# Two-layer GNN on one core: segment maxima subtracted by TensorE, scans in PSUM, and a regrouped division between the layers

## The chip, the cores and the metric

The kernel runs on one core of one Trainium2 chip. The metric is device time in microseconds (us). A core has TensorE (PE), VectorE (DVE), ScalarE (ACT), GpSimd (POOL) and SyncE (SP), each with its own instruction queue. They work on SBUF and PSUM and meet only through semaphores. Here SP issues the plain DMAs, and POOL issues the indirect ones (gathers of rows by an index list).

## The reference, cut to what matters

The graph has 6250 nodes with 128 numbers each and 106250 edges sorted by destination. Layer 0 is a softmax aggregation, separately for each of the 128 channels:

```python
h = maximum(layernorm(x), 0)
msg = h[src] + edge_attr                  # (106250, 128)
s = msg * beta
m = segment_max(s, dst)                   # (6250, 128)
e = exp(s - m[dst])
agg = segment_sum(msg * e, dst) / segment_sum(e, dst)
x = x + (agg @ H(phm_rule, W) + bias) + h
```

Layer 1 is a graph attention layer on `h = maximum(layernorm(x), 0)`: `Wx = h @ W.T` in 4 heads of 32, a logit for each edge and head, a softmax over each destination's edges, the weighted sum of `Wx[src]`, an elu, and a residual.

## The kernel before

Edges are taken in 208 groups of 512 (NG = 208, GE = 512, four blocks of 128). Each engine runs its own software pipeline over the groups (`sweep_edges`); a stage is listed with a lag, and the stages of one step stand on the engine's queue in the order of the list. An engine executes its queue strictly in order.

**Layer 0.** POOL issues four gathers a group (`gather0`, line 586) of `h` rows from DRAM into one of four ring buffers `ring_h`; it may run ahead until the ring is full (it waits for `lifted` of four groups back). ACT (merge0 lag 5, lift0 lag 0, weigh0 lag 3) copies the rows to PSUM (`lift0`, line 703), takes the exponentials of two groups of numbers from `bank[2]` (`weigh0`, lines 688 and 691), and merges finished sums into `acc` (`merge`, lines 666 to 674). DVE (add0 0, one_hot0 0, products0 3, maxima0 1) adds the rows to the edge attributes (line 950), builds a one-hot matrix (line 976), multiplies weights and messages (line 967), and finds segment maxima. For the maxima the messages stand transposed in PSUM (channels on partitions, edges along the row), and two scans run over them in `segment_max`: one forward (line 929) into `run_max`, one reversed (line 932) into `seg_max`, each with the flags of segment starts as its other tensor; line 939 takes the step between groups (`drop`), and line 960 subtracts the maxima from the messages into `diff`. PE (sums0 4, turn0 0, unturn0 2) transposes the messages by a product with `beta_ident` (`turn0`, line 1188), transposes `diff` back into `bank[2]` (`unturn0`, line 1197), and forms the segment sums by 16 multiplications with the one-hot matrices (`segment_sums`, line 1179). The merge of a group must end before the sums of the next may start.

An f32 multiplication of 128x128 by 128x128 appears in the records as two MATMULs. The lines of the trace speak of those halves, a row "x8" is four of them.

**Between the layers.** `acc` holds numerators and denominators for all nodes. In 13 batches of 512 nodes (the last has 106), ACT takes Ln of the denominator and twice Exp of the negative (`seed0`, lines 715 to 718), to PSUM and to SBUF; POOL multiplies that first guess of the reciprocal by the denominator (`polish0`, line 597); DVE makes the Newton step and multiplies by the numerator (`divide0`, lines 1008 and 1010); PE multiplies by the weight matrix on top of the bias (`layer_out`, lines 1219 and 1223; the bias is split in three bf16 parts by lines 991 to 999 on DVE); DVE adds to the nodes and takes statistics (`finish0`, lines 1019 and 800), two batches behind. `norm_all_nodes` then computes all reciprocal roots in Newton steps on DVE (lines 809 to 822), the same function as in the preamble. After it ACT normalizes, PE multiplies, and SP stores the table that layer 1 gathers from.

**Layer 1** has the same structure. `segment_max` is shared; there its data are 4 rows (heads) in PSUM and its forward scan writes to PSUM (`sums`).

Of the kernel before, what the change touches and what calls it, by code (L numbers as in the profile page):

```python
# [20 lines left out]
BF16 = mybir.dt.bfloat16  # L21
I32 = mybir.dt.int32
ALU = mybir.AluOpType
ACT = mybir.ActivationFunctionType

P = 128
# [44 lines left out]
def gnn_kernel(nc, x_in, src_in, dst_in, ea_in, rule_in, w0_in, bias_in, beta_in, w1_in, a_in, out):  # L71
# [31 lines left out]
    with ctx:  # L103
# [23 lines left out]
        head_pick = sb("head_pick", [P, H])  # L127
        junk = sb("junk", [1, 1])
# [3 lines left out]
        bias_parts = sb("bias_parts", [P, GB, D], BF16)  # L132
        ones_parts = sb("ones_parts", [P, P], BF16)
# [52 lines left out]
        run_max = sb("run_max", [P, 2, GE])  # L186
# [9 lines left out]
        bias_hi, bias_mid, bias_lo = (hn[:, 0, i, :].bitcast(BF16)[:, 0:D] for i in range(3))  # L196
        bias_rest = hn[:, 1, 0, :]
# [55 lines left out]
        bias_step = sem("bias_step")  # L253
        bias_made = sem("bias_made")
# [3 lines left out]
        mid_inv = sem("mid_inv")  # L258
# [77 lines left out]
        def _(sp):  # L336
# [122 lines left out]


# [11 lines left out]
            def load1(g, s, use):  # L472
                if s % HALF == 0:
                    load_lists(g, s, use, L1)
# [39 lines left out]
        def _(pool):  # L514
# [32 lines left out]
            pool.memset(ones_parts[:, :], 1.0).then_inc(self_pool, 1)  # L547
# [44 lines left out]
            def polish0(b):  # L592
                w = LAST if b == NBAT - 1 else GE
                pool.wait_ge(mid_seed, b + 1)
                if b >= 2:
                    pool.wait_ge(mid_inv, b - 1)
                pool.tensor_tensor(diff[:, b % 2, 0:w], acc[:, 1, b * GE:b * GE + w], ring_h[:, b % HRING, 0:w], ALU.mult  # L597
                                   ).then_inc(mid_near, 1)

            straight(NBAT, [(0, polish0)])  # L600
# [26 lines left out]
        def _(act):  # L627
# [25 lines left out]

            def merge(g, s, use, k, read_out, where=own_sums):
# [50 lines left out]
            sweep_edges(act, [(5, merge0), (0, lift0), (3, weigh0)])  # L705
# [3 lines left out]

            def seed0(b):  # L710
                w = LAST if b == NBAT - 1 else GE
                if b >= HRING:
                    act.wait_ge(mid_out, b - HRING + 1)
                near = ring_h[:, b % HRING, 0:w]
                act.activation(near, acc[:, 1, b * GE:b * GE + w], ACT.Ln).then_inc(mid_log, 1)
                act.wait_ge(mid_log, b + 1)
                act.activation(bank[b % HRING][:, 0:w], near, ACT.Exp, scale=-1.0)
                act.activation(near, near, ACT.Exp, scale=-1.0).then_inc(mid_seed, 1)

            straight(NBAT, [(0, seed0)])  # L720
# [63 lines left out]
        def _(dve):  # L784
# [21 lines left out]
            def norm_all_nodes():  # L806
# [52 lines left out]
            def h0(b, u, use):  # L859
                if u in DVE_SLOTS:  # L860
# [7 lines left out]
                    for t in range(GB):  # L868
                        ins = dve.tensor_scalar(run_max[:, 0, t * D:(t + 1) * D],
# [4 lines left out]
                    lnx = run_max[:, 0, :].rearrange("p (t d) -> p t d", d=D)  # L874
# [22 lines left out]

            dve.tensor_scalar(beta_ident[:, :], ident[:, :], beta[:, 0:1], None, ALU.mult).then_inc(beta_ready, 1)
# [18 lines left out]
            def segment_max(g, s, use, k, n, data):  # L917
                par = s % 2
                run = run_max[0:n, par, :] if k is L0 else head_run
                run_end = run_max[0:n, 1 - par, GE - 1:GE] if k is L0 else seg_max[0:n, 1 - par, GE - 1:GE]  # L920
# [10 lines left out]
                dve.wait_ge(k["scanned"], 2 * g + 1)  # L931
                dve.tensor_tensor_scan(seg_max[0:n, par, ::-1], flag[:, GE:0:-1], run[:, ::-1], -BIG,  # L932
# [21 lines left out]
            def maxima0(g, s, use):  # L954
                par = s % 2
                dve.wait_ge(L0["msgT"], g + 1)
                segment_max(g, s, use, L0, P, bank[par][:, :])
# [386 lines left out]
```

## Time and profile before

| | us |
|---|---|
| median of 3 runs | 2346.74 (2345.33 to 2385.2) |
| the profiled execution, its own time | 2345.14 |
| its span in the profile | 2343.4 |
| busy: PE / DVE / ACT / POOL | 1771.0 / 2109.2 / 1384.5 / 1644.0 |
| mean granted PE clock | 0.948 of full speed |

The profile is of one execution. Its times are us unless marked ns. PE is TensorE's multiplications and PEld its weight loads; SPq is a queue of SP. A line such as L586 is a line of the kernel before. In the lines of the trace, "busy" is the sum of a group, then comes the mean of one in ns, then the idle time of the engine just before them and what ended it; "issue" is idle time in which the engine waited for nothing that the profile shows. POOL's records of indirect DMAs are the time that it takes to issue them, not the transfer. Layer 0's gathers run from 67 to 1133 us, the piece between the last merge and the last statistics from 1155.3 to 1216.5, and layer 1's from 1251 us on.

### The profile page before, as it was taken

How to read it: one execution, taken by the hardware profiler on the slowest of the kernel's cores; microseconds unless marked ns; L12 is line 12 of the kernel's file. 1: busy time of each engine (PE TensorE's matmuls, PEld its weight loads, DVE VectorE, ACT ScalarE, POOL GpSimd, SP SyncE). 2: the span in 40 equal slices, each digit the busy share in tenths (PEclk: the TensorE clock that was granted, in tenths of full speed). 3: DMA queues.
4: the chain of work that ended last, by engine and by line, in shares of the span. 5: the costliest groups of instructions: out<-in, count | busy, mean ns of one | idle time of the engine just before them, and what ended most of it. 6: DMA issues, size and time to landing. Idle time of an engine off the chain costs nothing.

```text
span 2343.4 us, 60995 instructions
## 1 busy us (share of the span) xinstructions
PE 1771.0 (76%) x14105; PEld 1632.4 (70%) x14106; DVE 2109.2 (90%) x4081; ACT 1384.5 (59%) x3509; POOL 1644.0 (70%) x1728
## 2 busy tenths in 40 slices
PE   0466666666666666666557999999999999999996
PEld 0466666666666666666447888888888888888885
DVE  5799999999999999999666988889888888888887
ACT  2266666666666666666783555555555555555555
POOL 3677777777777777777314777777777777777772
PEclk9999999999999999999857999999999999999998
DMA  4544444444444444444003333333333333333332
GB/s 126 146 128 129 133 125 127 129 129 132 128 133 128 124 128 133 128 132 129 23 0 96 62 60 59 59 59 59 58 59 59 58 59 59 58 59 58 59 60 66
DMA packets 338882, 214.19 MB, mean 91 GB/s; under 512 B 170832, under 2 KB 305339, under 8 KB 338828
## 3 DMA queue, kind: packets, MB, share of 16 engines
q0 software_dynamic: 53248, 112.57, 20.8%
q1 hardware_dynamic: 285580, 101.01, 16.9%
q8 instruction: 22, 0.36, 0.1%
q14 instruction: 32, 0.26, 0.0%
HBM read 201.38 MB, written 10.30 MB: 90 GB/s over the span
## 4 chain that ended last, share of the span: by engine, by line
POOL 49%; issue 22%; DVE 14%; DMA 7%; PE 3%; ACT 2%; SPq 1%; POOLq 1%; DVEq 1%; ACTq 0%
POOL msg L608 26%; POOL ring_h L586 23%; DMA ring_h<-h_dram,meta_g 5%; DVE seg_max L932 3%; DMA msg<-wx_dram,meta_g 2%; DVE sums L929 2%; DVE run_max L929 2%; PE sums L1179 1%; DVE onehot L913 1%; DVE prod L967 1%; DVE msg L950 1%; DVE onehot L976 1%; DVE prod L1083 1%; ACT sums L703 1%; POOL diff L597 1%
## 5 line engine op out<-in xcount | busy, mean ns | idle before, releaser
L608 POOL DMA_INDIRECT msg<-wx_dram,meta_g x832 | 790.5, 950 | 292.6 <-issue 246.9
L586 POOL DMA_INDIRECT ring_h<-h_dram,meta_g x832 | 812.6, 977 | 259.5 <-issue 257.7
L1179 PE MATMUL sums<-onehot,prod 128*128 128x128 f32 x3312 | 690.3, 292 | 27.0 <-ACT acc L674 11.8
L1179 PE MATMUL sums<-onehot,wgt 128*128 128x128 f32 x3312 | 671.0, 286 | 0.0
L1179 PEld LDWEIGHTS sums<-onehot,prod 128*128 128x128 f32 x3312 | 531.9, 202 | 73.6 <-issue 71.3
L1179 PEld LDWEIGHTS sums<-onehot,wgt 128*128 128x128 f32 x3312 | 533.5, 203 | 0.0
L1188 PE MATMUL banks<-beta_ident,msg 128*128 128x128 f32 x1664 | 244.4, 291 | 342.8 <-DVE msg L950 342.8
L1188 PEld LDWEIGHTS banks<-beta_ident,msg 128*128 128x128 f32 x1664 | 204.6, 194 | 383.2 <-DVE msg L950 332.4
L674 ACT ACTIVATE acc<-sums 128x1022 f32 x412 | 421.6, 1023 | 0.1
L703 ACT ACTIVATE sums<-ring_h 128x512 f32<-128x512 f32 x208 | 125.2, 602 | 385.4 <-DMA ring_h<-h_dram,meta_g 385.3
L929 DVE TENSOR_TENSOR_SCAN sums<-flags,seg_max,banks 4x512 f32<-4x512 bf16 x207 | 264.0, 1276 | 5.2 <-PE banks L1277 3.7
L929 DVE TENSOR_TENSOR_SCAN run_max<-flags,run_max,banks 128x512 f32<-128x512 bf16 x207 | 263.4, 1272 | 0.0
L932 DVE TENSOR_TENSOR_SCAN seg_max<-flags,run_max 128x512 f32<-128x512 bf16 x208 | 254.7, 1224 | 7.1
L932 DVE TENSOR_TENSOR_SCAN seg_max<-flags,sums 4x512 f32<-4x512 bf16 x208 | 251.1, 1207 | 7.1
L666 ACT ACTIVATE carried<-acc,scale 128x2 f32 x414 | 120.9, 292 | 177.2 <-PE sums L1179 162.2
L1268 PEld LDWEIGHTS banks<-window,onehotT 128*128 128x128 f32 x1664 | 211.7, 199 | 3.4 <-ACT onehotT L751 2.8
L1268 PE MATMUL banks<-window,onehotT 128*128 128x4 f32 x1664 | 205.7, 247 | 2.2 <-DMA window<-wx_dram 2.2
L739 ACT ACTIVATE sums<-logit_d 128x16 f32<-128x16 f32 x208 | 39.0, 188 | 263.0 <-DVE logit_d L1075 262.0
L913 DVE TENSOR_SCALAR onehot<-iota_f,meta_g 128x128 f32<-128x128 f32 x832 | 182.7, 279 | 5.8 <-DMA meta_g<-meta 5.7
L950 DVE TENSOR_TENSOR msg<-msg,sums 128x512 f32<-128x512 f32 x208 | 141.1, 678 | 15.1 <-ACT sums L703 14.8
L967 DVE TENSOR_TENSOR prod<-sums,msg 128x512 f32<-128x512 f32 x208 | 141.9, 682 | 1.8 <-ACT sums L691 1.8
L976 DVE TENSOR_TENSOR onehot<-banks,meta_g 128x512 f32<-128x512 f32 x208 | 142.5, 685 | 0.0
(166 smaller groups left out, 2667.0 us busy)
## 6 DMA issues: line engine op xcount, KB each, us to landing
msg<-in_edge_attr SPq DMA_DIRECT2D x207, 256.0 KB, 2.9
flags<-flag_dram SPq DMA_DIRECT2D x52, 512.2 KB
ring_h<-h_dram,meta_g POOLq DMA_INDIRECT x832
msg<-wx_dram,meta_g POOLq DMA_INDIRECT x832
window<-wx_dram SPq DMA_DIRECT2D x832, 2.0 KB
wx_dram<-msg SPq DMA_DIRECT2D x13, 272.0 KB, 2.4
nodes<-in_x SPq DMA_DIRECT2D x4, 768.0 KB, 8.2
h_dram<-wgt SPq DMA_DIRECT2D x12, 256.0 KB, 2.2
```

The source lines that it names most:

```text
L586: pool.indirect_dma_start(hg[:, s % HRING, b, :], None, h_dram, bass.IndirectOffsetOnAxis(ap=meta_g[:, s, b:b + 1], axis=0)).then_inc(L0[" ...
L608: pool.indirect_dma_start(msg[:, s, b, :], None, wx_dram, bass.IndirectOffsetOnAxis(ap=meta_g[:, s, b:b + 1], axis=0)).then_inc(L1["gather ...
L674: act.activation(acc[:, :, bass.ds(node + 1, WIN - 1)], where[:, :, 1:WIN], ACT.Copy).then_inc(k["merged"], 1)
L913: ins = dve.tensor_scalar(onehot[:, s, b, :], iota_f[:, :], key[:, b:b + 1], None, ALU.is_equal)
L929: dve.tensor_tensor_scan(run, flag[:, 0:GE], data, before, ALU.add, ALU.max).then_inc(k["scanned"], 1)
L932: dve.tensor_tensor_scan(seg_max[0:n, par, ::-1], flag[:, GE:0:-1], run[:, ::-1], -BIG, ALU.add, ALU.max).then_inc(k["scanned"], 1)
L950: dve.tensor_tensor(msg[:, s, :, 0:D], msg[:, s, :, 0:D], row_psum.rearrange("p (b d) -> p b d", b=GB), ALU.add).then_inc(L0["added"], 1)
L967: dve.tensor_tensor(prod[:, s % 2, :, :], wgt_psum.rearrange("p (b d) -> p b d", b=GB), msg[:, s, :, 0:D], ALU.mult).then_inc(L0["multipli ...
L976: dve.tensor_tensor(onehot[:, s, :, :], steps, key, ALU.is_equal).then_inc(L0["onehots"], 1)
L1179: ins = pe.matmul(where[:, j, bass.ds(off, P)], what[:, slot, b, :], onehot[:, s, b, :], start=(b == 0), stop=(b == GB - 1), skip_group_ch ...
L1188: ins = pe.matmul(bank[s % 2][:, b * P:(b + 1) * P], msg[:, s, b, 0:D], beta_ident[:, :], start=True, stop=True)
L1268: ins = pe.matmul(bank[1][:, b * H:(b + 1) * H], onehotT[:, s % 2, b * P:(b + 1) * P], window[:, s, b, :], start=True, stop=True)
```

## The change

In layer 0 the forward scan writes in place over the transposed messages in PSUM, the reversed scan reads them there, and `diff` on DVE is gone. PE forms `beta * msg - maxima` itself in `bank[2]`: one multiplication of `beta_ident` with all 512 columns of messages, and four of the maxima with a negated identity added to it. Between the layers ACT takes the logarithms of batches 0 to 3 in one go, then their exponentials, then the logarithms of the other nine, then theirs, and copies POOL's product to PSUM; POOL multiplies twice a batch (denominator and numerator by the guess), DVE makes one instruction a batch, and the weight matrix is negated. The bias is added to the nodes by POOL, in 13 instructions after its last gather. One Ln on one number is issued ahead of the last merge. The Newton steps have three instructions in place of four. SP's first list for layer 1 is loaded at the end of layer 0.

```diff
@@ segment_max (DVE, both layers)
-                run = run_max[0:n, par, :] if k is L0 else head_run
-                run_end = run_max[0:n, 1 - par, GE - 1:GE] if k is L0 else seg_max[0:n, 1 - par, GE - 1:GE]
+                run = data if k is L0 else head_run
+                run_end = seg_max[0:n, 1 - par, GE - 1:GE]
...
                 dve.wait_ge(k["scanned"], 2 * g + 1)
+                if k is L0 and later(g, 2):
+                    dve.wait_ge(L0["unturned"], g - 1)
                 dve.tensor_tensor_scan(seg_max[0:n, par, ::-1], flag[:, GE:0:-1], run[:, ::-1], -BIG,
@@ maxima0 (DVE)
-                segment_max(g, s, use, L0, P, bank[par][:, :])
-                if later(g, 2):
-                    dve.wait_ge(L0["unturned"], g - 1)
-                dve.tensor_tensor(diff[:, par, :], bank[par][:, :], seg_max[:, par, :], ALU.subtract
-                                  ).then_inc(L0["shifted"], 1)
+                segment_max(g, s, use, L0, P, bank[s % 2][:, :])
@@ turn0, unturn0 (PE)
-                    pe.wait_ge(L0["shifted"], g - 1)
+                    pe.wait_ge(L0["scanned"], 2 * g - 2)
...
-                pe.wait_ge(L0["shifted"], g + 1)
                 if later(g, 1):
                     pe.wait_ge(L0["weighed"], g)
+                pe.matmul(bank[2][:, :].rearrange("p (b d) -> p b d", b=GB), beta_ident[:, :], msg[:, s, :, 0:D],
+                          start=True, stop=False, skip_group_check=True)
+                pe.wait_ge(L0["scanned"], 2 * g + 2)
                 for b in range(GB):
-                    ins = pe.transpose(bank[2][:, b * P:(b + 1) * P], diff[:, s % 2, b * P:(b + 1) * P], ident[:, :])
+                    ins = pe.matmul(bank[2][:, b * P:(b + 1) * P], seg_max[:, s % 2, b * P:(b + 1) * P], neg_ident[:, :],
+                                    start=False, stop=(b == GB - 1), skip_group_check=True)
@@ layer_out (PE)
-                pe.matmul(sums[0:rows, b % 2, 0, 0:t * D], ones_parts[:, 0:rows],
-                          bias_parts[:, 0:t, :].rearrange("p t d -> p (t d)"), start=True, stop=False, skip_group_check=True)
...
-                                    ring_h[:, b % HRING, i * P:i * P + rows], phm[:, :, :].rearrange("p j b -> p (j b)"),
-                                    start=False, stop=(i == t - 1), skip_group_check=True)
+                                    ring_h[:, b % HRING, i * P:i * P + rows], phm_neg[:, :], start=True, stop=True)
@@ POOL, after its last gather0 (waits for the nodes of the first residual), in place of polish0
+            def add_bias(b):
...
+                pool.tensor_tensor(tiles, tiles, bias_all[:, :].rearrange("p (a d) -> p a d", a=1).to_broadcast([P, t, D]),
+                                   ALU.add).then_inc(bias_added, 1)
+            straight(NBAT, [(0, add_bias)])
+            def near0(b):
...
+                pool.wait_ge(mid_seed, b + 1)
+                if b >= 2:
+                    pool.wait_ge(mid_lifted, b - 1)
+                pool.tensor_tensor(diff[:, b % 2, 0:w], acc[:, 1, b * GE:b * GE + w], seed, ALU.mult).then_inc(mid_near, 1)
+                pool.wait_ge(mid_near, b + 1)
+                pool.tensor_tensor(seed, acc[:, 0, b * GE:b * GE + w], seed, ALU.mult).then_inc(mid_quot, 1)
@@ ACT, end of layer 0 and between the layers, in place of seed0
-            sweep_edges(act, [(5, merge0), (0, lift0), (3, weigh0)])
+            sweep_edges(act, [(5, merge0), (0, lift0), (3, weigh0)], until=NG + 4)
+            act.activation(spare[:, :], spare[:, :], ACT.Ln)
+            last(merge0, 0)
...
+            def log0(b):            # Ln of acc[:, 1] into free buffers
+            def seed0(b):           # waits mid_log, and mid_out of batch b - 4; Exp(-log) into ring_h
+            def lift_near0(b):      # waits mid_near, and mid_agg of batch b - 4
+                act.activation(bank[b % HRING][:, 0:w], diff[:, b % 2, 0:w], ACT.Copy).then_inc(mid_lifted, 1)
+            for b in range(HRING):
+                log0(b)
+            for b in range(HRING):
+                seed0(b)
+            for b in range(HRING - 1):
+                lift_near0(b)
+            for b in range(HRING, NBAT):
+                log0(b)
+            lift_near0(HRING - 1)
+            for b in range(HRING, NBAT):
+                seed0(b)
+                if b > HRING:
+                    lift_near0(b - 1)
+            lift_near0(NBAT - 1)
@@ DVE, between the layers, in place of divide0
+            def quotient0(b):
...
+                dve.scalar_tensor_tensor(rows, bank[b % HRING][:, 0:w], 2.0, rows, ALU.subtract, ALU.mult).then_inc(mid_agg, 1)
@@ norm_all_nodes (DVE), three times
-                    link(dve.tensor_tensor(t, y, y, ALU.mult))
+                    link(dve.scalar_tensor_tensor(t, y, -0.5, y, ALU.mult, ALU.mult))
                     link(dve.tensor_tensor(t, t, v, ALU.mult))
-                    link(dve.tensor_scalar(t, t, -0.5, 1.5, ALU.mult, ALU.add))
-                    link(dve.tensor_tensor(y, y, t, ALU.mult))
+                    link(dve.scalar_tensor_tensor(y, t, 1.5, y, ALU.add, ALU.mult))
@@ SP, after layer 0's loads
+            sp.wait_ge(L0["onehots"], NG)
+            for q in range(HRING):
+                sp.wait_ge(L0["gathered"][q], 64 * (NG // HRING))
+            load_lists(0, 0, 0, L1)
```

## Rows read from the trace of the kernel before

**Rows 1.** The page: busy time, share of the span, and instructions.

```profile
PE 1771.0 (76%) x14105; PEld 1632.4 (70%) x14106; DVE 2109.2 (90%) x4081; ACT 1384.5 (59%) x3509; POOL 1644.0 (70%) x1728
```

**Rows 2.** Windows: stretch, length, engines' busy time, granted clock, DMA share, GB/s.

```profile
67.00:1133.00 1066.00, 714.49 (x5722) 660.91 (x5723) 1033.77 (x1444) 661.96 (x1628) 812.64 (x832) 1.00 0.46 128
1155.30:1216.50 61.20, 28.72 (x111) 23.59 (x111) 35.17 (x88) 55.45 (x65) 13.46 (x13) 0.53 0.00 0
1251.00:2343.00 1092.00, 987.53 (x8002) 913.92 (x8002) 959.30 (x2332) 619.97 (x1693) 798.16 (x838) 0.92 0.32 59
```

**Rows 3.** Lines of layer 0, 67 to 1133 us: busy, mean ns, idle before.

```profile
L586 POOL DMA_INDIRECT ring_h<-h_dram,meta_g x832 | 812.6, 977 | 259.5 <-issue 257.7 <-ACT sums L703 1.8
L929 DVE TENSOR_TENSOR_SCAN run_max<-flags,run_max,banks 128x512 f32<-128x512 bf16 x204 | 259.6, 1272 | 0.0
L932 DVE TENSOR_TENSOR_SCAN seg_max<-flags,run_max 128x512 f32<-128x512 bf16 x205 | 251.0, 1224 | 7.0
```

**Rows 4.** In order of time, layer 0: start, duration, engine, line.

```profile
602.73 0.94 POOL L586 DMA_INDIRECT ring_h<-h_dram,meta_g  x1 [0.30 <-issue]
603.05 1.22 DVE L932 TENSOR_TENSOR_SCAN seg_max<-flags,run_max 128x512 f32<-128x512 bf16 x1
603.98 1.05 POOL L586 DMA_INDIRECT ring_h<-h_dram,meta_g  x1 [0.30 <-issue]
...
604.45 0.69 DVE L960 TENSOR_TENSOR diff<-banks,seg_max 128x512 f32<-128x512 f32 x1
...
605.05 0.68 DVE L950 TENSOR_TENSOR msg<-msg,sums 128x512 f32<-128x512 f32 x1
```

**Rows 5.** Lines of layer 1, 1300 to 2300 us.

```profile
L608 POOL DMA_INDIRECT msg<-wx_dram,meta_g x793 | 753.6, 950 | 241.7 <-issue 235.3 <-DVE prod L1083 6.4
...
L929 DVE TENSOR_TENSOR_SCAN sums<-flags,seg_max,banks 4x512 f32<-4x512 bf16 x199 | 253.8, 1276 | 4.0 <-PE banks L1277 2.6 <-issue 0.4
L932 DVE TENSOR_TENSOR_SCAN seg_max<-flags,sums 4x512 f32<-4x512 bf16 x200 | 241.5, 1207 | 6.9
```

**Rows 6.** In order of time, TensorE in one group of layer 0.

```profile
605.78 1.16 PE L1188 MATMUL banks<-beta_ident,msg 128*128 128x128 f32 x8 [1.36 <-DVE msg L950]
...
606.77 0.60 PE L1197 MATMUL banks<-ident,diff 128*128 128x128 f32 x4
...
607.33 0.46 PE L1179 MATMUL sums<-onehot,prod 128*128 128x128 f32 x2
...
608.96 0.39 PE L1179 MATMUL sums<-onehot,wgt 128*128 128x128 f32 x2
```

**Rows 7.** In order of time: last gather, last lift, and after the last merge.

```profile
1131.93 0.94 POOL L586 DMA_INDIRECT ring_h<-h_dram,meta_g  x1 [0.30 <-issue]
...
1135.65 0.60 ACT L703 ACTIVATE sums<-ring_h 128x512 f32<-128x512 f32 x1 [2.93 <-DMA ring_h<-h_dram,meta_g]
...
1155.29 1.28 ACT L715 ACT_TABLE_LOAD   x1
```

**Rows 8.** Lines between the layers; line 717 has the same row.

```profile
L715 ACT ACT_TABLE_LOAD x13 | 16.7, 1283 | 0.2
```

**Rows 9.** In order of time: one batch of 512 nodes between the layers.

```profile
1190.51 1.28 ACT L715 ACT_TABLE_LOAD   x1
...
1191.70 0.70 DVE L1008 SCALAR_TENSOR_TENSOR banks<-diff,banks 128x512 f32<-128x512 f32 x1 [1.41 <-POOL diff L597]
...
1193.82 0.87 DVE L800 BATCH_NORM_STATS2 stats<-nodes 128x6 f32<-128x128 f32 x4
...
1194.92 1.28 ACT L715 ACT_TABLE_LOAD   x1
...
1194.97 1.09 POOL L597 TENSOR_TENSOR diff<-acc,ring_h 128x512 f32<-128x512 f32 x1 [3.31 <-ACT ring_h L718]
```

**Rows 10.** In order of time: two dependent instructions of the Newton steps.

```profile
1220.95 0.19 DVE L820 TENSOR_SCALAR newton<-newton 128x49 f32<-128x49 f32 x1
1221.18 0.21 DVE L821 TENSOR_TENSOR norm<-norm,newton 128x49 f32<-128x49 f32 x1
```

More of the change, by code:

```diff
@@ L131, in gnn_kernel @@
         bias_all = sb("bias_all", [P, D])
[L132 to L133 removed]
+        phm_neg = sb("phm_neg", [P, D])
+        spare = sb("spare", [1, 1])
         rule_rep = sb("rule_rep", [P, PH, PH])
@@ L195, in gnn_kernel @@
         onehotT = sb("onehotT", [P, 2, GE])
-        bias_hi, bias_mid, bias_lo = (hn[:, 0, i, :].bitcast(BF16)[:, 0:D] for i in range(3))
-        bias_rest = hn[:, 1, 0, :]
+        log_rows = msg[:, :, :, :].rearrange("p r b t -> p (r b t)")
         res = onehot[:, 0:FIN, :, :].rearrange("p s b d -> p s (b d)")
@@ L472, in load1 @@
             def load1(g, s, use):
-                if s % HALF == 0:
+                if s % HALF == 0 and later(g, 1):
                     load_lists(g, s, use, L1)
@@ L590, in _ @@
             sweep_edges(pool, [(0, gather0)])
-            def polish0(b):
+            for u in range(WXB):
+                if u not in DVE_SLOTS:
+                    pool.wait_ge(ln0_sum[u], (NBAT - 1 - u) // WXB + 1)
+            pool.wait_ge(ln0_part, 3 * sum(b % WXB in DVE_SLOTS for b in range(NBAT)))
+            def add_bias(b):
+                t = 1 if b == NBAT - 1 else GB
+                tiles = nodes[:, b * GB:b * GB + t, :]
+                pool.tensor_tensor(tiles, tiles, bias_all[:, :].rearrange("p (a d) -> p a d", a=1).to_broadcast([P, t, D]),
+                                   ALU.add).then_inc(bias_added, 1)
+            straight(NBAT, [(0, add_bias)])
+            def near0(b):
                 w = LAST if b == NBAT - 1 else GE
+                seed = ring_h[:, b % HRING, 0:w]
                 pool.wait_ge(mid_seed, b + 1)
                 if b >= 2:
[L596 to L600, printed above, removed]
+                    pool.wait_ge(mid_lifted, b - 1)
+                pool.tensor_tensor(diff[:, b % 2, 0:w], acc[:, 1, b * GE:b * GE + w], seed, ALU.mult).then_inc(mid_near, 1)
+                pool.wait_ge(mid_near, b + 1)
+                pool.tensor_tensor(seed, acc[:, 0, b * GE:b * GE + w], seed, ALU.mult).then_inc(mid_quot, 1)
+            straight(NBAT, [(0, near0)])
             def gather1(g, s, use):
@@ L1022, in finish0 @@
                 statistics(b)
-            for u in range(WXB):
-                if u not in DVE_SLOTS:
-                    dve.wait_ge(ln0_sum[u], (NBAT - 1 - u) // WXB + 1)
-            straight(NBAT, [(0, divide0), (2, finish0)])
+            straight(NBAT, [(0, quotient0), (2, finish0)])
             dve.wait_ge(measured, 2 * NBAT)
```

68 lines of the change are left out of this document (28 added, 40 removed).

## The prediction

> **What bounds the kernel now.** I read the page first, then the windows of the two layers and of the piece between them, then the lines of each, then single groups in order of time. The page makes VectorE look like the bound (90% busy) with GpSimd at 70% [rows 1]. The window of layer 0 says the same: VectorE is busy 1033.77 of 1066 us, GpSimd 812.64, TensorE 714.49 at a granted clock of 1.00 [rows 2]. 208 groups in 1066 us make 5.125 us a group.
>
> GpSimd's 70% is misleading. Its busy time in layer 0 is 832 gathers, and the idle time ahead of them is 257.7 us of "issue", in which it waited for nothing [rows 3]: 812.6 + 257.7 = 1070 us, all of the window. So both engines are full, and the question is which sets the period. In one group, a gather that starts at 602.73 takes 0.94 us and the next starts 1.25 us after it; the one that starts at 603.98, inside the reversed scan (line 932, 603.05 to 604.27), takes 1.05 [rows 4]. The longer one delays all that follows. Four gathers at 1.25 would take 5.00 us; the mean gather of 977 ns against 944 for a plain one adds 4 x 0.033 = 0.13, which gives 5.13, the period seen. In layer 1 the same scan reads PSUM (sums) in place of run_max, and there the mean gather is 950 ns although the scans run as long [rows 5]. My reading: VectorE, with a cycle of 5.1 us, sets the period, and GpSimd, which could do 5.00, is pushed into step once a group by a scan with both inputs in SBUF. The Trainium skill (SBUF — State Buffer, "SBUF: two separate sides") says that a Vector instruction with two SBUF inputs holds a port pair against GpSimd for its whole duration. By that rule the gather of 603.98 would end 0.94 after 604.27, at 5.21; it ended at 5.03, so the trace agrees on who blocks and not on the length. By the rule's "two SBUF inputs" the changed scan blocks nobody.
>
> **Layer 0.** Removed: the subtraction on VectorE, 0.69 us; it starts at 604.45, and the next instruction at 605.05, so it occupies 0.60 [rows 4]. The scans now write and read PSUM in place. The trace prices both: the forward scan takes 1276 ns into PSUM against 1272 into SBUF, the reversed one 1207 from PSUM against 1224 from SBUF [rows 3, 5]. That is from 4 partitions, at the same 512 elements; I take nothing. VectorE's cycle falls to 5.1 - 0.6 = 4.5. If the PSUM access cost 0.1 a scan at 128 partitions it would be 4.7, still under 5.00.
>
> Then the gathers are next: 5.00 us a group, and nothing here makes them shorter. The small drop of line 939, with SBUF operands only, stays, so I take 5.01. Gain: (5.125 - 5.01) x 208 = 24 us. Bounds: 26 at 5.00; nothing if the scan still blocks.
>
> Added is TensorE work. Now a group starts turn0 at 605.78, unturn0 0.99 later, the sums 0.56 after that, and their last pair starts 1.63 on and needs 0.22 [rows 6]: 3.40 us. The four transposes (0.44) become one 512-column multiplication and four 128-column ones. The latter have turn0's form: eight halves whose pace is 0.11 to 0.12, 0.89. The 512-column one isn't in the trace. Below: as many columns at turn0's pace, 4 x 0.22 = 0.89. Above: four records of line 1188 with their full length, 4 x 0.29 = 1.16 [rows 6]. I take 0.89, since TensorE works by columns and a long row can't pace worse than four short ones. Sum 0.99 + 0.89 + 0.89 + 0.13 of gap + 1.85 = 4.75 us. It fits under 5.01 with 0.26 to spare. With all added pieces at record length (1.16 each) it is 5.29 and TensorE is the bound. The Trainium skill (TensorE: Matmul & The Clock Gate, "Wait — 56ns, not 53.3ns?") gives 216 ns for 512 columns; four passes are an estimate of 0.86 and a sum of 4.72.
>
> The order inside a group allows it. With the gather's landing as 0: lift 0.6, weights of g-3 by 1.8, add by 1.4; turn0 1.8 to 2.8; the new multiplication waits for weighed (1.8) and runs to 3.7; the scans of g-2 are long done; the subtraction ends by 4.6; sums0 of the next step waits for the merge (under 4.0) and ends by 6.5; turn0(g+1) wants to start at 6.8. Behind TensorE's wait for the scan stands only sums0, whose inputs are no later. VectorE's new wait for unturned(g-2) is met before the step starts.
>
> **End of layer 0.** From the last gather's landing (lift at 1135.65) to the table load that follows the last merge (1155.29) it is a chain of four sums and merges in turn, 19.6 us [rows 7]. unturn0 stands ahead of the first of them and is 1.3 longer: +1. POOL's 13 bias additions (about 1.1 each, 14 us) start after its last gather at 1131.93 + 0.94 and end before 1155; VectorE's nine bias instructions vanish from under the same cover. The early Ln (one table load) falls into ScalarE's wait for the last sums.
>
> **Between the layers.** 12 full batches of 4.41 us: ScalarE alternates Ln and Exp, with two table loads of 1283 ns in each batch, 26 in all [rows 8, 9]. The period 1190.51 to 1194.92 is 2.57 of loads and 1.84 of three activations, 0.61 each. The piece takes 61.2 us [rows 2]. After, in us from the last merge: Ln of batches 0 to 3, 2.3 (0.61 each, overlapping a little); load 1.3; first Exp done at 4.2. GpSimd then multiplies twice a batch: 2 x 1.09 [rows 9] + 2 x 0.07 of semaphore (VectorE's dependent instructions show 0.04 [rows 10]; for GpSimd I take more) = 2.32. Batch 2's first product ends at 10.0, its lift at 10.7; then load 1.3, nine logarithms 4.5, lift 0.6, load 1.3, Exp 0.6: batch 4 starts at 19.0 (GpSimd idles some 5). Eight batches x 2.32 = 18.6: 37.6. VectorE's own batch is 0.70 + 0.68 + 0.87 [rows 4, 9] and waits, 2.3, with finish0 two batches behind, so about 6.7 more: 44.3. Saved 61.2 - 44.3 = 17. ScalarE is then at 1.2 a batch and no bound. Bounds: 2.0 a batch and overlapping activations give 20; GpSimd at 2.7 a batch gives 13. The Trainium skill (ScalarE: Activation LUTs, "Table sets: the hidden batching unit") says that one set holds both ln and exp and that ln then exp costs one load, of some 2.7. By that rule grouping saves no load and the piece gains only the second Exp; the trace has 26 loads of 1.28, so the measurement decides.
>
> The Newton steps lose three instructions, 0.23 from start to start each [rows 10]: -0.7 here and -0.7 in layer 0's preamble, both on the path. The hoisted list load lands while the table's last stores do: -0.2. Layer 1 is unchanged.
>
> **Sum.** Against the profiled execution's own 2345.14 (span 2343.4, 1.7 outside it): -24 + 1 - 17 - 1.4 - 0.2 = -41.6, 2303.5. The median stands 1.6 above that execution: 2305.
>
> **Rivals.**
> - TensorE becomes the bound (ends slower). It decides from 5.125 us a group, that is once the subtraction costs 0.37 more than I have. At 5.29 layer 0 ends (5.29 - 5.01) x 208 = 58 later than forecast: 2363. For: [rows 6] leave 0.26. Against: the paces there. If the clock also fell as in layer 1 (0.92 [rows 2]) the 4.75 would be 5.16, and the time 2336. Layer 0 has 1.00 now and gets more columns; the skill's page on TensorE ("What's actually happening") calls the slow state the idle one, and by it this fall doesn't come.
> - The gathers are still pushed, because the scan and not its second SBUF input does it. Then layer 0 stays at 5.125: 2305 + 24 = 2329. Against: layer 1's 950 ns [rows 5].
> - The change between the layers doesn't do what it says: GpSimd, ScalarE and VectorE wait for each other in a ring, 3.0 us a batch instead of 2.32. 11 x 0.7 = 8 more: 2313.
> - Everything lands at its favourable bound: 26 and 20 and no tail: 2299, just past 2%.
>
> **How the numbers follow.** Forecast 0.60, with its own range 2299 to 2312; favourable end and beyond 0.15; TensorE as bound 0.09 (0.05 of it to 2336 or so, 0.04 above the old time); gathers still pushed 0.07; the ring between the layers 0.09. The range 2295 to 2332 leaves out the slow TensorE case and little else. 2% is 46.9 us, about what a measurement of this kernel can tell from no change: faster means under 2299.8. Faster 0.17, same 0.79, slower 0.04.
>
> **What would show it.** In layer 0: GpSimd at 4 x 1.25 with nearly all gathers at 0.94, also during reversed scans; VectorE with about 0.5 us of idle time a group, released by ScalarE's lift; TensorE about 95% occupied, clock 1.00. Between the layers: four table loads, products at 2.3 us a batch, 44 us from the last merge to the last statistics. It is wrong if VectorE's adds still wait for nothing, if ScalarE's lift waits less for the gathers' landing and more for "added", or if TensorE shows no gap ahead of turn0.

## The result and the profile after

The changed kernel takes 2317.5 us, the median of 4 runs (2316.5 to 2318.2), beside 2346.7 for the kernel before (2345.3 to 2347.8, a fourth run at 2385.2 in a slower state left out): a ratio of 0.9876, 95% interval 0.9856 to 0.9895. It is faster by 29 us, 1.2%, where 42 were forecast. The gain is clear of zero and under the 2% that the prediction asks of "faster", so it is "same", to which 0.79 was given.

The page after, busy times (as [rows 1]):

```profile
PE 2008.5 (87%) x15340; PEld 1798.4 (78%) x15341; DVE 1997.7 (86%) x3847; ACT 1363.9 (59%) x3488; POOL 1648.2 (71%) x1754
```

VectorE fell from 90% to 86% and TensorE rose from 76% to 87%. Where the time went is read from the marks between the stages. Each mark is the start or end of one instruction in the two traces, and the last is the span's end:

| us | before | after | difference | forecast |
|---|---|---|---|---|
| up to layer 0's first gather | 67.0 | 67.0 | -0.1 | -0.7 |
| first to last gather of layer 0 | 1065.9 | 1038.6 | -27.3 | -24 |
| last gather's end to last merge's end | 22.4 | 37.1 | **+14.7** | +1 |
| last merge to last statistics | 61.2 | 44.5 | -16.8 | -17 |
| last statistics to first gather of layer 1 | 34.7 | 34.7 | 0.0 | -0.9 |
| layer 1 | 1092.2 | 1094.3 | +2.1 | 0 |

The two large terms came out near the forecast. One small term, the end of layer 0, is wrong by 14 us. The other differences (3 us better in layer 0, 4 us worse in the rest) about cancel, so those 14 us are the size of the miss.

The windows after: stretch, length, the engines' busy time (PE, PEld, DVE, ACT, POOL), granted clock, DMA share, GB/s. They answer to [rows 2]; the second is new.

```profile
67.00:1105.50 1038.50, 953.66 (x6953) 827.76 (x6954) 925.72 (x1237) 670.17 (x1628) 785.23 (x832) 1.00 0.46 132
1110.00:1120.00 10.00, 0.00 (x0) 0.00 (x0) 10.00 (x1) 1.44 (x4) 10.00 (x9) 0.53 0.00 0
1142.60:1187.00 44.40, 23.99 (x98) 20.64 (x98) 26.55 (x75) 24.58 (x42) 28.70 (x26) 0.56 0.00 1
1221.70:2316.00 1094.30, 983.39 (x7994) 909.84 (x7994) 955.80 (x2322) 618.94 (x1691) 799.69 (x838) 0.93 0.31 59
```

**Layer 0.** VectorE is now busy 925.7 of 1038.5 us, and it has idle time. The groups of instructions after (busy, mean ns, idle before them and what ended it), as [rows 3]:

```profile
L591 POOL DMA_INDIRECT ring_h<-h_dram,meta_g x832 | 785.3, 944 | 259.9 <-issue 254.8
...
L977 DVE TENSOR_TENSOR_SCAN banks<-flags,seg_max,banks 128x512 f32<-128x512 bf16 x207 | 264.8, 1279 | 0.0
L982 DVE TENSOR_TENSOR_SCAN seg_max<-flags,banks 128x512 f32<-128x512 bf16 x208 | 253.8, 1220 | 7.2
...
L1000 DVE TENSOR_TENSOR msg<-msg,sums 128x512 f32<-128x512 f32 x208 | 143.0, 687 | 94.6 <-ACT sums L728 87.0
```

The mean gather is 944 ns where it was 977, and VectorE waits 0.45 us a group for ScalarE's lift, thus for the gathers: the bound has passed from VectorE to GpSimd. The scans in PSUM cost what they cost in SBUF at 128 partitions too: 1279 against 1272, 1220 against 1224. TensorE in one group, in order of time, as [rows 6]:

```profile
605.30 1.15 PE L1212 MATMUL banks<-beta_ident,msg 128*128 128x128 f32 x8 [1.09 <-DVE msg L1000]
606.29 1.02 PE L1219 MATMUL banks<-msg,beta_ident 128*128 128x512 f32 x2
607.15 1.05 PE L1223 MATMUL banks<-neg_ident,seg_max 128*128 128x128 f32 x8
608.05 0.39 PE L1203 MATMUL sums<-onehot,prod 128*128 128x128 f32 x2
...
609.61 0.39 PE L1203 MATMUL sums<-onehot,wgt 128*128 128x128 f32 x2
609.83 1.15 PE L1212 MATMUL banks<-beta_ident,msg 128*128 128x128 f32 x8
```

From start to start 0.99 + 0.86 + 0.90 + 1.78 = 4.53 us, with no wait in this group. That is under the gathers' 4.99.

**End of layer 0.** In order of time, the last gather, GpSimd's bias additions, and what VectorE and TensorE do meanwhile:

```profile
1104.55 0.94 POOL L591 DMA_INDIRECT ring_h<-h_dram,meta_g  x1 [0.30 <-issue]
...
1105.52 15.08 POOL L605 TENSOR_TENSOR nodes<-nodes,bias_all 128x512 f32<-128x512 f32 x13
1105.86 1.22 DVE L982 TENSOR_TENSOR_SCAN seg_max<-flags,banks 128x512 f32<-128x512 bf16 x1
...
1107.11 13.10 DVE L989 SCALAR_TENSOR_TENSOR drop<-seg_max,flags 128x1 f32<-128x1 f32 x1
...
1120.13 0.68 DVE L1000 TENSOR_TENSOR msg<-msg,sums 128x512 f32<-128x512 f32 x1
...
1120.86 2.08 PE L1212 MATMUL banks<-beta_ident,msg 128*128 128x128 f32 x8 [12.68 <-DVE msg L1000]
```

The step between groups (line 989) works on one column and takes 0.22 us as a rule. Here it takes 13.10, from 1107.11 to 1120.21, and GpSimd's 13 additions run to 1120.60. The `x13` row hides that they touch: 15.08 us for 13 instructions, each recorded from 0.03 to 0.06 us before the end of the one ahead. The step ends 0.02 after the twelfth addition (1120.19). The thirteenth, a short one of 0.44 on 128 columns, follows as closely as the others, and here the step got in. VectorE's queue stands behind the step, and TensorE waits 12.68 us for the last group's messages. When it resumes, eight halves take 2.08 us instead of 1.15. The window from 1110 to 1120 shows it idle at a granted clock of 0.53; from 1120 to 1123 the clock is 0.50, the lower level of 1.2 GHz, and from 1126 it is 1.00 again. Against the first run below, where nothing holds the step, the last group's multiplications start 11.3 us later, and the other 3 us of the 14 are slower work of TensorE behind them (its clock is at 0.50 once more from 1139 to 1141). The chain of waits isn't much help: it gives the hole as 10.26 us of "issue", since nothing in it is a semaphore.

**Between the layers.** GpSimd's products, as the last line of [rows 9]:

```profile
1146.83 1.09 POOL L616 TENSOR_TENSOR diff<-acc,ring_h 128x512 f32<-128x512 f32 x1 [26.23 <-ACT ring_h L746]
1148.00 1.27 POOL L618 TENSOR_TENSOR ring_h<-acc,ring_h 128x512 f32<-128x512 f32 x1
...
1161.61 1.09 POOL L616 TENSOR_TENSOR diff<-acc,ring_h 128x512 f32<-128x512 f32 x1 [5.14 <-ACT ring_h L746]
...
1164.00 1.09 POOL L616 TENSOR_TENSOR diff<-acc,ring_h 128x512 f32<-128x512 f32 x1
```

The first product starts 4.24 us after the last merge, batch 4 at 19.0, and a batch takes 2.40: 4.2, 19.0 and 2.32 were forecast.

### The profile page after: what moved, and what is told of

Its sections match the earlier page's. It is cut to its first block, busy times and chain, and to the rows that moved or that the text cites. A ratio compares the mean times of both kernels' runs of the same rounds, so it can differ in the third digit from the quotient of the medians.

```text
span 2316.0 us, 63521 instructions
## 1 busy us (share of the span) xinstructions
PE 2008.5 (87%) x15340; PEld 1798.4 (78%) x15341; DVE 1997.7 (86%) x3847; ACT 1363.9 (59%) x3488; POOL 1648.2 (71%) x1754
## 4 chain that ended last, share of the span: by engine, by line
POOL 45%; issue 21%; DMA 13%; DVE 9%; PE 5%; ACT 4%; SPq 1%; POOLq 0%; DVEq 0%; ACTq 0%
POOL msg L628 25%; POOL ring_h L591 20%; DMA ring_h<-h_dram,meta_g 10%; DMA msg<-wx_dram,meta_g 2%; DVE sums L977 2%; PE sums L1203 2%; DVE seg_max L982 2%; ACT sums L728 2%; DVE onehot L961 1%; DVE prod L1107 1%; ACT acc L699 1%; POOL ring_h L618 1%; POOL diff L616 1%; PE banks L1212 0%; SPq L488 0%
## 5 line engine op out<-in xcount | busy, mean ns | idle before, releaser
L591 POOL DMA_INDIRECT ring_h<-h_dram,meta_g x832 | 785.3, 944 | 259.9 <-issue 254.8
L1223 PEld LDWEIGHTS banks<-neg_ident,seg_max 128*128 128x128 f32 x1664 | 219.5, 192 | 100.4 <-issue 99.9
L977 DVE TENSOR_TENSOR_SCAN banks<-flags,seg_max,banks 128x512 f32<-128x512 bf16 x207 | 264.8, 1279 | 0.0
L982 DVE TENSOR_TENSOR_SCAN seg_max<-flags,banks 128x512 f32<-128x512 bf16 x208 | 253.8, 1220 | 7.2
L1223 PE MATMUL banks<-neg_ident,seg_max 128*128 128x128 f32 x1664 | 220.1, 275 | 0.0
L1219 PE MATMUL banks<-msg,beta_ident 128*128 128x512 f32 x416 | 214.7, 598 | 0.3 <-ACT sums L716 0.3
L787 ACT ACTIVATE sums<-logit_d 128x16 f32<-128x16 f32 x208 | 39.1, 188 | 270.6 <-DVE logit_d L1099 265.8
```

What stands on the lines that cost most here:

```text
L591: pool.indirect_dma_start(hg[:, s % HRING, b, :], None, h_dram, bass.IndirectOffsetOnAxis(ap=meta_g[:, s, b:b + 1], axis=0)).then_inc(L0[" ...
L977: dve.tensor_tensor_scan(run, flag[:, 0:GE], data, before, ALU.add, ALU.max).then_inc(k["scanned"], 1)
L1219: pe.matmul(bank[2][:, :].rearrange("p (b d) -> p b d", b=GB), beta_ident[:, :], msg[:, s, :, 0:D], start=True, stop=False, skip_group_che ...
L1223: ins = pe.matmul(bank[2][:, b * P:(b + 1) * P], seg_max[:, s % 2, b * P:(b + 1) * P], neg_ident[:, :], start=False, stop=(b == GB - 1), s ...
```

## The experiments

The theories after the result. **A**: the additions shut VectorE's step out, because it reads two tensors of SBUF while GpSimd's instructions follow each other without a gap. Rival **B**: the additions aren't the cause, and the tail is long because TensorE's added work or its clock made it so. On layer 0: the gain comes from the gathers no longer being pushed (theory) or from VectorE's removed subtraction alone (rival **C**), and TensorE has room (theory) or is nearly the bound (rival). The expectations below use such letters too, each in its own words. Beside each time stands the stretch from the last gather's end to the last statistics, the two middle rows of the table, which is 83.6 us before and 81.5 after.

### The additions held until VectorE's last step

```diff
             for u in range(WXB):
...
+            pool.wait_ge(L0["dropped"], NG)
             straight(NBAT, [(0, add_bias)])
```

> The changed kernel, with one wait more on GpSimd: the 13 bias additions start only when VectorE's last drop (line 989) is done. Theory A (the last-but-one drop, whose operands are all in SBUF, is shut out by the additions for 13.1 us and everything behind it on VectorE is late): the drop takes 0.2 us again, the end of layer 0 shortens by 12 to 13 us, and the additions still end before the first product between the layers: 2305. Rival B (the end of layer 0 is longer because TensorE's chain is longer or its clock falls): no change, 2317.

Measured: 2302.7 us (ratio to the kernel before in the same runs 0.9816, 95% interval 0.9800 to 0.9832; so below too). The stretch is 67.4 us, 14 less than after. In order of time:

```profile
1118.63 0.22 DVE L990 SCALAR_TENSOR_TENSOR drop<-seg_max,flags 128x1 f32<-128x1 f32 x1
...
1119.03 15.14 POOL L605 TENSOR_TENSOR nodes<-nodes,bias_all 128x512 f32<-128x512 f32 x13 [11.81 <-DVE drop L990]
1134.39 1.09 POOL L617 TENSOR_TENSOR diff<-acc,ring_h 128x512 f32<-128x512 f32 x1 [0.22 <-ACT ring_h L747]
```

Nothing waits for the additions although they start 13.5 us later: they end at 1134.17, just ahead of the first product. B falls.

### Each half of the change alone

The kernel before with only layer 0's part:

```diff
-                run = run_max[0:n, par, :] if k is L0 else head_run
+                run = data if k is L0 else head_run
...
-                dve.tensor_tensor(diff[:, par, :], bank[par][:, :], seg_max[:, par, :], ALU.subtract
-                                  ).then_inc(L0["shifted"], 1)
...
+                pe.matmul(bank[2][:, :].rearrange("p (b d) -> p b d", b=GB), beta_ident[:, :], msg[:, s, :, 0:D],
+                          start=True, stop=False, skip_group_check=True)
```

> The kernel before, with only the layer 0 part of the change (subtraction on TensorE, scans in PSUM); middle, bias and Newton steps as before. Theory A: layer 0 gains 27 at its gathers and loses 1 at its end, since no bias additions stand there: 2347 - 26 = 2321. Rival B (the end of layer 0 loses some 13 through the new TensorE work itself): 2333.

Measured: 2322.0 us (0.9897, 0.9881 to 0.9914). The stretch is 84.6, one more than before: the +1 that the prediction had for TensorE's longer part of the last steps.

The changed kernel with that part undone, so with the additions and the new division:

```diff
-                run = data if k is L0 else head_run
+                run = run_max[0:n, par, :] if k is L0 else head_run
...
+                dve.tensor_tensor(diff[:, par, :], bank[par][:, :], seg_max[:, par, :], ALU.subtract
+                                  ).then_inc(L0["shifted"], 1)
```

> The changed kernel with its layer 0 part undone (subtraction on VectorE, forward scan into SBUF), so the middle, the bias additions on GpSimd and the Newton steps alone. Theory A: the gathers run at 5.12 a group as before; the middle gains 17 and the Newton steps 1.4, but the additions shut out a scan or a drop with SBUF inputs for 12 to 13: 2347 - 5 = 2342. Rival B (the additions harm nothing, the loss is TensorE's): 2347 - 18 = 2329.

Measured: 2343.7 us (0.9987, 0.9977 to 0.9998). The division saves 17 and the additions take nearly all of it back: the stretch is 81.8, 1.9 under before. Here another instruction of VectorE is caught, the reversed scan, whose two inputs are in SBUF in this kernel. It too gets in behind the twelfth addition, and the thirteenth, short one now takes 1.36 us where it took 0.44:

```profile
1129.85 16.00 POOL L606 TENSOR_TENSOR nodes<-nodes,bias_all 128x512 f32<-128x512 f32 x13
...
1131.71 13.91 DVE L981 TENSOR_TENSOR_SCAN seg_max<-flags,run_max 128x512 f32<-128x512 bf16 x1
```

In the changed kernel the same scan reads PSUM and takes 1.22 under the same additions (above, 1105.86). For the scan, where the operands lie decides.

### The step between groups with one tensor

```diff
-                    dve.scalar_tensor_tensor(drop[0:n, s:s + 1], run_end, seg_max[0:n, par, 0:1],
-                                             flag[:, 0:1], ALU.subtract, ALU.add).then_inc(k["dropped"], 1)
+                    dve.tensor_scalar(drop[0:n, s:s + 1], flag[:, 0:1], run_end, seg_max[0:n, par, 0:1],
+                                      ALU.add, ALU.subtract).then_inc(k["dropped"], 1)
```

> The changed kernel with the drop written with one tensor operand from SBUF (the flag) and the two maxima as scalar pointers; the additions stay where they are. If it is the second SBUF tensor that needs the port shared with GpSimd, the drop takes 0.2 us under the additions and the time is 2305, as in the run with the wait. If any SBUF operand is shut out, it stays at 13 us and 2317.

Measured: 2313.8 us (0.9865, 0.9849 to 0.9882), 4 under after and not the 12 expected. The stretch did what A says, 67.4 us, with the additions where they were:

```profile
1105.35 15.15 POOL L605 TENSOR_TENSOR nodes<-nodes,bias_all 128x512 f32<-128x512 f32 x13
...
1106.94 0.27 DVE L989 TENSOR_SCALAR drop<-flags,seg_max 128x1 f32<-128x1 bf16 x1
```

But layer 1 grew from 1094.3 to 1104.2 us. `segment_max` is shared, and there the new form takes 260 ns for 207 and the mean gather rises from 952 to 964 ns. So the same form in layer 0 only:

```diff
+                    if k is L0:
+                        dve.tensor_scalar(drop[0:n, s:s + 1], flag[:, 0:1], run_end, seg_max[0:n, par, 0:1],
+                                          ALU.add, ALU.subtract).then_inc(k["dropped"], 1)
+                    else:
```

> The changed kernel with the one-tensor drop in layer 0 alone; layer 1 keeps the old form. In the run with the new form in both layers the end of layer 0 was 14 us shorter and layer 1 was 10 us longer (its drop took 260 ns in place of 207). If layer 1's loss came from its own drop: layer 1 back at 1094 to 1097 and 2303 in all. If it came from anything else (where layer 1 starts, for one): 2313.

Measured: 2301.3 us (0.9810, 0.9794 to 0.9827); layer 1 is back at 1093.7, mean gather 952. Layer 1's loss was its own step's form. The step itself grew by 0.05 us a group and the period of the gathers by about as much. Read one by one, without the first and last ten groups, the gathers over 0.96 us are 87 in the changed kernel and 119 with the new form, and all of the 87 and 115 of the 119 start while the one-hot comparisons (line 961) run, which follow the step. A comparison reads one tensor, so two tensors of SBUF aren't needed to lengthen a gather.

### A wait between the additions

```diff
                 pool.tensor_tensor(tiles, tiles, bias_all[:, :].rearrange("p (a d) -> p a d", a=1).to_broadcast([P, t, D]),
                                    ALU.add).then_inc(bias_added, 1)
+                pool.wait_ge(bias_added, b + 1)
```

> The changed kernel, with GpSimd waiting after each bias addition for its own semaphore, so that the additions no longer overlap one another by 0.03 to 0.06 us but leave a gap. If the drop is shut out because the next addition always holds the port before the last lets go, it gets in at the first gap, takes about 1.3 us at most, and the time is 2306. If GpSimd wins each time whatever the gap, it stays at 13 us: 2318.

This run, and those marked "on the other chip" below, were on a chip where the kernels took 1.3 to 1.5 times as long (before itself 3270 us, 3252 to 3294). 3384 us (1.0336, 1.0284 to 1.0388) is thus not the 2306 or 2318 expected and says nothing on the few us in question; the changed kernel wasn't run there. Single instructions of VectorE and GpSimd took what they take on the other chips (between 300 and 1000 us the scans 1279 and 1221 ns, a gather 945; TensorE's were longer, at a granted clock of 0.86), and those do speak:

```profile
1595.59 16.66 POOL L605 TENSOR_TENSOR nodes<-nodes,bias_all 128x512 f32<-128x512 f32 x13
```

```profile
1596.62 0.26 DVE L990 SCALAR_TENSOR_TENSOR drop<-seg_max,flags 128x1 f32<-128x1 f32 x1
...
1603.36 0.25 DVE L990 SCALAR_TENSOR_TENSOR drop<-seg_max,flags 128x1 f32<-128x1 f32 x1
...
1609.33 1.05 DVE L990 SCALAR_TENSOR_TENSOR drop<-seg_max,flags 128x1 f32<-128x1 f32 x1
```

The 13 additions take 16.66 us for 15.08, and the wait leaves a gap of 0.08 after each. All three steps, two tensors each, ran under them, took 0.26, 0.25 and 1.05 us instead of 13.10, and each ended 0.01 to 0.02 after an addition did. The last waited for less than one addition. So the additions as such don't shut VectorE out for long: with a small gap between them they don't. That the gap alone is what matters isn't shown, since the step of the changed kernel and the scan above got in ahead of the thirteenth addition, where there is none.

### The forward scan into SBUF

Only the place of one tensor changes; the subtraction stays on TensorE, and VectorE's work stays short. First on the other chip, then again:

```diff
-                run = data if k is L0 else head_run
+                run = diff[0:n, par, :] if k is L0 else head_run
```

> The changed kernel, with layer 0's forward scan written to SBUF and the reversed scan reading it there (two SBUF inputs again), subtraction still on TensorE, so VectorE's cycle stays at 4.5 us. Theory A (two causes: the shorter VectorE cycle and the freed port): gathers issued during a reversed scan are longer than 0.94 again and the period is above 5.00, 5.05 to 5.3: 2329 to 2380. Rival C (only VectorE's cycle counted, the long gathers were a symptom of being in step with it): 4.99 to 5.01 and 2317 to 2320.

On the other chip: 3252 us (0.9938, 0.9905 to 0.9971), mean gather 1088 ns. The long gathers of theory A are there, but not its loss of time: this is 132 us less than the changed kernel with waits between the additions took on that chip (3384), and nearly all of it in layer 0's gathers (1398 us for 1529). The granted clock between 300 and 1000 us was 0.90 for 0.86. Something other than GpSimd's issue bounds layer 0 there; what, is open.

> The changed kernel, with layer 0's forward scan written to SBUF and the reversed scan reading it there; subtraction still on TensorE, so VectorE's cycle stays at 4.5 us. Theory A (two causes: the shorter VectorE cycle and the freed port): gathers during a reversed scan are longer than 0.94 and the period is above 5.00, somewhere in 5.05 to 5.6: 2329 to 2440. Rival C (only VectorE's cycle counted, the long gathers were a symptom of being in step with it): 4.99 to 5.01 and 2317 to 2320.

Measured: 2446.5 us (1.0437, 1.0419 to 1.0454), 129 more than after and 101 more than before, somewhat above the range of theory A. The lines of 300 to 1000 us, and in order of time one scan and the gather that starts in it:

```profile
L591 POOL DMA_INDIRECT ring_h<-h_dram,meta_g x495 | 549.5, 1110 | 150.9 <-issue 150.3 <-ACT sums L728 0.6
```

```profile
608.87 1.22 DVE L982 TENSOR_TENSOR_SCAN seg_max<-flags,diff 128x512 f32<-128x512 bf16 x1
...
609.29 1.56 POOL L591 DMA_INDIRECT ring_h<-h_dram,meta_g  x1 [0.30 <-issue]
```

Four gathers take 4 x (1.110 + 0.305) = 5.66 us, the period of that window (700 us for 495/4 groups). The gather ends 0.76 us after the scan, as the one of [rows 4] did (605.03 against 604.27). The difference is when it starts: there 0.29 us ahead of the scan's end, here 0.80. That holds for all of layer 0 (without the first and last ten groups): every gather over 1.0 us starts inside a reversed scan and ends 0.75 to 0.77 after it, in the kernel before and here, and in the changed kernel no gather is that long. Rival C falls: shorter VectorE work without the freed operand makes the kernel slower than it was. The converse, the freed operand with the subtraction left on VectorE, wasn't run.

### The 512-column multiplication twice

```diff
+                pe.matmul(bank[2][:, :].rearrange("p (b d) -> p b d", b=GB), beta_ident[:, :], msg[:, s, :, 0:D],
+                          start=True, stop=True, skip_group_check=True)
                 pe.matmul(bank[2][:, :].rearrange("p (b d) -> p b d", b=GB), beta_ident[:, :], msg[:, s, :, 0:D],
```

> The changed kernel, with the 512-column product of beta_ident and the messages done twice (the first result is overwritten). From the trace of the changed kernel TensorE needs 4.53 us a group when nothing holds it (605.30 to 609.83); one product more is 0.86: 5.39, now above GpSimd's 4.995, so TensorE is the bound and layer 0 lasts 82 longer: 2400. By the 4.75 of the prediction it would be 5.61 and 2445. If TensorE were not near the bound at all, 2317.

On the other chip: 3462 us (1.0579, 1.0501 to 1.0657); no answer in time.

> The changed kernel, with the 512-column product of beta_ident and the messages done twice. TensorE's 4.53 us a group (start to start where nothing holds it) grow by 0.86 to 5.39, above GpSimd's 4.995: layer 0 lasts 82 longer, 2400. By the 4.75 of the prediction it would be 5.61 and 2445. If TensorE were far from being the bound: 2317.

Measured: 2380.0 us (1.0147, 1.0126 to 1.0167), where 2400 was expected from 4.53 us a group. The window from 300 to 1000 us:

```profile
300.00:1000.00 700.00, 700.00 (x4769) 573.82 (x4769) 603.69 (x794) 437.60 (x1061) 500.97 (x532) 1.00 0.44 125
```

TensorE is busy all of the time and now sets the period: VectorE's 794 instructions, six a group, make 132.3 groups, 5.29 us each. Less the 0.86 that was added, that is 4.43 for the changed kernel, near the 4.53 read above and under the 4.75 of the prediction. So about half a microsecond a group was free.

### Together, and better than both

The layer 0 step with one tensor, and ScalarE's first logarithms moved among the last merges, batch 0's ahead of the last but one and the next ones ahead of the last (every node has an edge to itself, so the last three groups can't touch those nodes), the others spread between the copies. First with the step's form in both layers, on the other chip:

```diff
-            sweep_edges(act, [(5, merge0), (0, lift0), (3, weigh0)], until=NG + 4)
...
+            sweep_edges(act, [(5, merge0), (0, lift0), (3, weigh0)], until=NG + 3)
...
+            act.wait_ge(L0["merged"], NG - 2)
+            log0(0)
+            last(merge0, 1)
```

> The changed kernel with the one-tensor drop, the logarithms of batches 0 to 3 moved ahead of the last merges into ScalarE's waits, and the other nine logarithms spread between the lifts so that GpSimd waits less ahead of batch 4. Expected: 12.5 less at the end of layer 0, 2.3 less ahead of the first Exp, 3 less ahead of batch 4: 2299. If the one-tensor drop does not help: 2312. If the logarithms delay the last merges instead of hiding there: 2302 or more.

On the other chip: 3366 us (1.0300, 1.0222 to 1.0378), which settles no time. In its trace the last merge to GpSimd's last product takes 33.4 us and GpSimd idles 1.63 us ahead of batch 4, where it was 5.14. Then with the form in layer 0 only, and batch 4's logarithm early too:

> As the run before this one, and in addition the logarithms of batches 0 to 4 ahead of the last two merges and the other eight between the lifts. From a trace of nearly this middle: the last merge to GpSimd's last product 33.4 us in place of 39.1. Expected 2303 - 6 = 2297. If the early logarithms delay the last merge: 2299 or more.

Measured: **2297.7 us** (2296.1 to 2298.8; ratio 0.9794, 0.9777 to 0.9810), the best of all. The stretch is 63.2 us for 67.7 without the moved logarithms: the last merge ends 1.6 later, and the piece behind it takes 38.4 for 44.4. GpSimd in order of time:

```profile
1131.45 1.09 POOL L616 TENSOR_TENSOR diff<-acc,ring_h 128x512 f32<-128x512 f32 x1 [11.71 <-ACT ring_h L741]
...
1142.38 1.09 POOL L616 TENSOR_TENSOR diff<-acc,ring_h 128x512 f32<-128x512 f32 x1 [1.30 <-ACT ring_h L741]
```

## Why the prediction was right in direction and 13 us off

**Layer 0: right, in size and mechanism.** The forecast had 5.01 us a group, set by gathers of 0.94 that nothing pushes; it is 1038.6/208 = 4.99. VectorE's idle time of 0.45 a group, released by ScalarE's lift, is the sign that was named (0.5), and TensorE's clock stayed at 1.00. The scan into SBUF shows that the freed operand is needed: with it undone, what VectorE gained in time is worth less than nothing. How much it would give alone isn't shown. VectorE was busy 1033.77/208 = 4.97 us of 5.125 in the kernel before, so an estimate is 0.13 us a group at most.

**TensorE: the term was too large, harmlessly.** 4.75 was forecast, 4.53 measured. The multiplications came out at 0.99, 0.86 and 0.90 (forecast 0.99, 0.89, 0.89). The sums were 1.78, not 0.13 + 1.85: I had added the gap ahead of them, and taken 1.63 from the first pair to the last, where the pace without a wait gives 1.56 (608.05 to 609.61). The rival "TensorE becomes the bound" thus had less behind it than the chance of 9 in 100 that it got; its mechanism is real, as the doubled multiplication shows, but it begins half a microsecond further on.

**End of layer 0: the step that failed.** "POOL's 13 bias additions start after its last gather and end before 1155" was a check of the wrong thing, whether they end in time, and I put them at nothing. They did end in time (1120.6), and cost 14 us: the end of layer 0 is 37.1 with them and 22.9 with them held behind the step. What they use together with VectorE I did not ask, some paragraphs after arguing on that very sharing in the other direction. The row was in view: the step of line 939 has all its operands in SBUF, and the prediction says so itself. From the trace of before its price could have been bounded: at 0 below, at the 14 us of all additions above. The likeliest value would not have been 2305 alone. As it stands, 2317.5 lies outside the likeliest case's 2299 to 2312. That the whole range of 2295 to 2332 held it is in part luck: its upper end was there for gathers that are still pushed (2329), which didn't happen, and no case on the list had this loss. Without this loss the changed kernel measured 2301.3 and 2302.7, inside the likeliest case's own range of 2299 to 2312.

The Trainium skill (SBUF — State Buffer, "SBUF: two separate sides") says that of a VectorE instruction with two SBUF inputs and a GpSimd instruction that reads SBUF, the one that starts first holds the pair for its instruction, and the other blocks. By that rule the step waits for the running addition, at most 1.28 us. The run with waits between the additions agrees (1.05 at most); the changed kernel doesn't (13.10, past the ends of ten additions), and there the measurement decides.

**Between the layers: right.** 44.5 us against 44.3. The products run at 2.40 a batch for 2.32, since the in-place one takes 1.27 and not 1.09, so GpSimd ends 39.1 us after the last merge and not 37.6, and the tail of TensorE and VectorE behind it is 5.3 for 6.7. The rival of a ring of waits at 3.0 a batch doesn't show.

**Newton steps and the list load: no effect on the path.** -1.6 was forecast for the preamble, the piece after the statistics and the load together; the marks moved by 0.1. The price held: the steps got shorter, from 5.10 us to 4.44 in both places. Their effect on the path, which the prediction took as given, doesn't show. After the statistics the same work behind them then took longer: VectorE's last copy of the table ends 24.7 us after the steps before and 25.3 after, with longer waits for TensorE. In the preamble the load of the first list is issued 0.5 earlier (62.73 for 63.27), and the first gather only 0.1. Why is open. Layer 1 took 2.1 us more, unchanged as it is. Its length was 1092.2 to 1096.9 in the kernels that leave it alone (those on the slow chip aside), so 2 us lie within what one profiled execution can tell.

## What to carry to other kernels

Work that is moved to an idle engine "under cover" needs two answers, not one: whether it ends in time, and what it shares with whoever is on the path meanwhile. On this chip look for VectorE instructions that read two tensors of SBUF, however small, and GpSimd work back to back beside them; move the work behind the last such instruction, or turn one tensor into a pointer operand there and only there. And when an operand is moved to PSUM, ask whose instructions it frees: here the deleted instruction without the freed operand made the kernel 101 us slower than it was, and both together 29 us faster.

## What the runs showed of the hardware that I had not expected

- A VectorE instruction on 128x1 with two SBUF tensors waited 13.10 us behind GpSimd additions that follow each other without a gap, and the reversed scan 13.91 less its own 1.22. Both were let in ahead of the last addition, the only short one (0.44 us where the others have 1.25), though it touches too. Gaps of 0.08 us after each addition let the same step end 0.25 to 1.05 after its start. Why VectorE isn't let in between two long additions that touch is open.
- The same step with one tensor and two pointer operands from SBUF ran in 0.27 us under the additions. Alone it is dearer than the other form (260 ns for 207 on 4 partitions), and in layer 1 the mean gather went from 952 to 964 ns. The long gathers there start while the one-hot comparisons run (all 87 of the changed kernel), instructions with one tensor of 128x128 from SBUF; why the step's form makes them more frequent is open.
- A gather's issue that is held by a scan with two SBUF inputs ends 0.75 to 0.77 us after that scan, and lasted up to 1.93 us. How much it loses depends on where in the scan it starts: those that start inside one took 1.07 us in the mean where VectorE set the period (before) and 1.55 where GpSimd did (scan into SBUF), for 0.94 elsewhere.
- On one chip the kernels took 1.3 to 1.5 times as long with the same durations of single instructions on VectorE and GpSimd, and a lower granted clock of TensorE (0.86 between 300 and 1000 us of the run with waits, where the changed kernel has 1.00). Times don't carry over from it, not even their order (the scan into SBUF), but who blocks whom can be read there.
